# Cross-attention and routed experts on one Trainium2 core: where VectorE adds the residual in the third slot of a block

## What is computed

```python
def rms_norm(x, w):                       # over the last axis (head of 128)
    return w * x * rsqrt(mean(x * x) + 1e-6)
q = (layernorm(x) @ Wq).reshape(B, S, 16, 128)
k = (ctx @ Wk).reshape(B, S, 4, 128)
v = (ctx @ Wv).reshape(B, S, 4, 128)
q, k = rms_norm(q, q_norm_w), rms_norm(k, k_norm_w)
probs = softmax(q @ k.T / sqrt(128))      # four query heads share one key head
x = x + (probs @ v).reshape(B, S, 2048) @ Wo
xn2 = layernorm(x)                        # 8192 tokens
w, sel = top_2(softmax(xn2 @ gate_w.T))   # of 12 experts, capped list for each
for each expert e: h = silu((xs @ w1.T) * (xs @ w3.T)) @ w2.T; x[tokens] += w * h
```

## Time and profile before

| | |
|---|---|
| median of 3 runs | 2482.19 us (2481.06 to 2484.36) |
| the profiled execution | 2481.01 us, span 2479.1 us |
| PE busy | 2271.0 us, 92% of the span |
| DVE busy | 1869.0 us, 75% |
| ACT busy | 1766.7 us, 71% |
| POOL busy | 1125.1 us, 45% |
| mean granted TensorE clock | 0.961 |

### The profile page before, as it was taken

How to read it: one execution, slowest core, us unless ns; L and a number is a source line. 1 busy time by engine, 2 the same in 40 slices (tenths; PEclk the granted TensorE clock), 3 DMA queues, 4 the chain that set the end, 5 groups by cost and what they waited for, 6 DMA issues and landing times. The chain is left out here.

```text
span 2479.1 us, 54081 instructions
## 1 busy us (share of the span) xinstructions
PE 2271.0 (92%) x12931; PEld 1152.0 (46%) x12931; DVE 1869.0 (75%) x5158; ACT 1766.7 (71%) x6911; POOL 1125.1 (45%) x1949
## 2 busy tenths in 40 slices
PE   3899999999999999999999999999999999468884
PEld 1344444444444444444444444445444444244442
DVE  6778888888888888888888888888888887436554
ACT  5877777777777777777777777777777777234442
POOL 4334444444444444444444444444444443268875
PEclk9899999999999999999999999999999999778886
DMA  8477766666777667676676777667676766359997
GB/s 256 94 140 138 140 139 138 136 134 137 136 144 141 137 137 144 138 137 137 137 136 135 135 142 143 136 135 141 140 139 137 136 135 119 83 144 188 182 177 93
DMA packets 894363, 348.08 MB, mean 140 GB/s; under 512 B 829004, under 2 KB 829260, under 8 KB 894288
## 3 DMA queue, kind: packets, MB, share of 16 engines
q1 hardware_dynamic: 867520, 297.06, 60.3%
q0 software_dynamic: 22912, 43.16, 9.8%
q10 hardware_dynamic: 3888, 7.38, 0.8%
HBM read 91.37 MB, written 57.71 MB: 60 GB/s over the span
## 5 line engine op out<-in xcount | busy, mean ns | idle before, releaser
L824 PE MATMUL pb<-wo,o 128*128 128x512 f16 x3072 | 709.8, 381 | 61.6 <-DVE work L1164 50.3
L954 ACT ACTIVATE work<-pb,small 128x128 f32<-128x128 f32 x1024 | 455.2, 453 | 165.1 <-DVE small L1139 165.1
L1407 POOL TENSOR_TENSOR small<-small 128x4 f32<-128x4 f32 (+1 forms) x584 | 485.4, 835 | 54.0 <-POOL small L1478 13.8
L824 PEld LDWEIGHTS pb<-wo,o 128*128 128x128 f16 x3072 | 287.1, 98 | 397.5 <-issue 61.2
L1478 POOL TENSOR_TENSOR small<-small 128x4 f32<-128x4 f32 x256 | 84.2, 329 | 697.3 <-ACT junk_q L935 691.6
L755 PE MATMUL pb<-wq,xT 128*128 128x512 f16 x1536 | 356.4, 382 | 0.9 <-DVE q L1127 0.9
L755 PE MATMUL pb<-wq,wkv_raw 128*128 128x512 f16 x1536 | 352.4, 379 | 0.6 <-DVE q L1127 0.6
L1127 DVE SCALAR_TENSOR_TENSOR q<-pb,small,q 128x128 f16<-128x128 f32 x1024 | 288.3, 344 | 71.7 <-ACT q L944 71.7
L968 ACT ACTIVATE o<-pb 128x512 f16<-128x512 f32 x256 | 153.1, 598 | 222.4 <-PE pb L812 221.8
L944 ACT ACTIVATE q<-pb,small 128x128 f16<-128x128 f32 x1024 | 291.1, 365 | 4.6 <-DMA qT<-q 4.5
L935 ACT ACTIVATE junk_q<-pb 128x128 bf16<-128x128 f32 x1024 | 273.4, 305 | 6.4 <-PE pb L755 6.4
(11 more groups left out here) (152 smaller groups left out, 3546.1 us busy)
## 6 DMA issues: line engine op xcount, KB each, us to landing
work<-x SPq DMA_DIRECT2D x128, 256.0 KB, 3.0
work<-c SPq DMA_DIRECT2D x64, 256.0 KB, 4.0
out<-work SPq DMA_DIRECT2D x64, 256.0 KB, 2.1
xn_scratch<-work SPq DMA_DIRECT2D x64, 256.0 KB, 2.3
wo_raw<-wo ACTq DMA_DIRECT2D x4, 1024.0 KB, 9.1
qT<-q SPq DMA_TRANSPOSE x256
pT<-p SPq DMA_TRANSPOSE x256
wq_raw<-wq ACTq DMA_DIRECT2D x3, 1024.0 KB, 11.3
```

Source lines behind the costliest of these rows:

```text
L824: mm = nc.tensor.matmul(WO_B[:, :], o16[:, HPG * a + h, :], part(O0 + g, b_)[:, h, :], start=(g == 0 and h == 0 and n == 0), stop=(g == NG ...
L954: ex = nc.scalar.activation(probs[:, cols], S_B[:, cols], ACT.Exp, bias=nmax[:, h:h + 1], scale=esc, accum_out=psums[:, h:h + 1])
L1407: return nc.gpsimd.tensor_tensor(out_, in_, neghalf[:, 0:n], ALU.pow)
```

## The change

On DVE, in the third slot of a block (g 2), `residual(b - 1)` stands ahead of `norm_k(b + 1)` and so also ahead of `normalise(b, 2)`; before, it stood behind both. Nothing else is touched: the same instructions with the same waits, on DVE alone.

```diff
                         if g == 1 and live(b):
                             split_v(b)
+                        if g == 2 and live(b - 1):
+                            residual(b - 1)
                         if g == 2 and live(b + 1):
                             norm_k(b + 1)
...
                         if g == 1 and live(b + 2):
                             stats_x(b + 2)
-                        if g == 2 and live(b - 1):
-                            residual(b - 1)
                         if live(b):
                             split_p(*cur)
```

## The result

| | before | with the change |
|---|---|---|
| median of 4 runs | 2481.62 us (2480.93 to 2484.36) | 2422.28 us (2419.59 to 2425.45) |
| profiled execution, span | 2481.01, 2479.1 | 2425.45, 2423.6 |
| start of the last residual | 2144.38 | 2086.48 |
| from there to the end | 334.7 | 337.1 |

The ratio is 0.9759, with a 95% interval of 0.9742 to 0.9777: 59.3 us faster by the medians, 55 to 64 by the interval. The forecast was 57.5 us faster, at 2424.7, in a range of 2421 to 2437.

What follows compares the result with a forecast made beforehand. PE was taken to bound the attention stage; 52.2 us from 60 waits, 1.74 from block 1, 1.43 at the loop's end and 2.16 from block 63 sum to 57.5, giving 2424.7 us, range 2421 to 2437.

Steps and rivals of the forecast that it cites:

- PE's wait: Third slot, ahead of out_project: PE's wait for the residual goes, 0.87 us a pass, with 1.4 us to spare.
- How often: Of PE's 63 waits, 60 alike give 52.2 us; block 1 gives 1.74 and the slot at the loop's end 1.43.
- Block 63: Last block, without norm_k: the residual passes normalise alone and PE starts out_project 2.16 us earlier, all taken as won.
- lower end of the range: Block 63's out_project at full clock with less idle time ahead, 1.3 us more, and 1.2 us run spread: about 2422.
- The sum: Whole kernel: 52.2 + 1.74 + 1.43 + 2.16 = 57.5 us won, giving 2424.7 us against the median.
- ACT and DVE behind the residual: Third slot: L1148 and ACT's p cast 0.3 us later, k cast waits for norm_k, delays don't add; DVE still waits 0.3 us.
- Can DVE hold the faster pace?: DVE's own chain a pass: 30.63 us, 30.9 with the delay, against PE's 31.45; PE stays the bound with 0.5 to spare.
- The second rival: DVE becomes the bound as the third slot grows over 0.5 us more than reckoned; 2453 us, chance 0.12.
- Is the residual's own input there?: Load of x_res, issued at 1016.99, has landed by 1019.1, over 4 us ahead of the residual's new start at 1023.42.
- the fourth rival: At the third slot's head the residual waits for its load, holding up DVE's chain; slower, 2524 us in its example, chance 0.03.
- POOL beside DVE: POOL's factor chain will run beside norm_k and L1148; slowing of DVE taken as 0, with 1.0 us a pass as other end.
- The third rival: PE doesn't go faster without its pause, from instruction queue refill or a lower clock; 2482 us within 0.2%, chance 0.05.

Runs made afterwards that it cites:

- halved run: Kernel before, with the residual in its new place only in blocks with odd b, in its old place in the others; ratio 0.9872, pass 31.88 us.
- run with the POOL products: The change, with 16 small POOL products (128x1) added behind the factor chain of the third slot; ratio 0.9762, pass 31.45 us.
- run of n = 3: The change, with three more unread bn_stats operations (128x512) on DVE ahead of its third slot's last operation; ratio 0.9975, pass 32.27 us.

## Why the prediction was right, and where not

*PE's wait.* Right by its own numbers: 0.87 us a pass was forecast, and 32.32 - 31.45 is 0.87. The 1.4 us to spare can be read in the rows after: the residual ends at 997.41 + 0.74 = 998.15 and PE starts at 999.68, 1.53 us later, of which 0.15 is the distance kept where PE does wait. That the residual need only be in time is shown by the run in which it comes 1.03 us later at no cost. The run with one more DVE operation goes to the edge: in block 36 the load held the residual up 1.47 us, and PE started 0.20 us behind the small matmul, in place of 0.03:

```profile
1251.47 0.75 DVE L1167 SCALAR_TENSOR_TENSOR work<-pb,small,work 128x512 f32<-128x512 f32 x1 [1.47 <-DMA work<-x]
```
```profile
1252.17 0.17 PE L844 MATMUL pb<-macc,ones_b 128*128 128x24 bf16 x1
1252.37 2.75 PE L825 MATMUL pb<-wo,o 128*128 128x512 f16 x12
```

*How often.* The halved run shows that the waits add up one by one. Block 1 too: PE's `out_project` of its third slot came 19.37 us behind that of its first slot in the kernel before (102.40 to 121.77), and 17.62 us with the change (101.55 to 119.17), 1.75 against a forecast of 1.74.

*Block 63.* Its `out_project` follows that of block 62 at 29.23 us instead of 31.49, 2.26 us won against a forecast of 2.16. I took all of it as kept. In this profile 0.4 us are given back in the next slot:

```profile
2066.62 4.39 PE L824 MATMUL pb<-wo,o 128*128 128x512 f16 x12 [1.99 <-DVE work L1164]
...
2074.02 2.76 PE L824 MATMUL pb<-wo,o 128*128 128x512 f16 x12 [1.64 <-DVE o L1076]
```

The twelve matmuls take 4.39 us where they took 4.03, and it is 7.40 us to the next group, not 6.99. The granted clock over the twelve is 0.61, against 0.67 before; singly they take 0.38 us at the one level and 0.63 at the other. But this can't be put down to the change. Over the fourteen traces the same twelve take 4.03 to 5.28 us with the residual in its old place and 2.75 to 5.13 in the new one. The 2.75, at a clock of 1.00 and with 5.71 us to the next group, is in the run with the POOL products:

```profile
2067.70 2.75 PE L825 MATMUL pb<-wo,o 128*128 128x512 f16 x12 [1.99 <-DVE work L1165]
```

So the further 1.3 us that I put at the lower end of the range do occur, in one of nine traces, and the clock granted at this place moves the distance to the next group between 5.7 and 8.4 us, whatever the kernel.

*The sum.* By the two profiles the last residual is 57.9 us earlier. Of these 0.85 lie ahead of block 1 and are no work of the change; 57.05 are, against 57.5. The experts' stage took 2.4 us more in this profile, and so the spans differ by 55.5. It moves by itself: the two profiles and the twelve others put it at 322 to 337 us. The medians differ by 59.3 us, inside the same scatter.

*ACT and DVE behind the residual.* L1148 came 0.25 us later (0.3 forecast), and ACT's k cast waits 0.49 us for the keys. The two delays don't add, and DVE still waits for PE, 0.34 us (0.3 forecast).

*Can DVE hold the faster pace?* This is the step that was mis-sized: "32.32 - 1.69 = 30.63 us", and with the delay 30.9, with 0.5 us to spare. It is 30.4, with 1.0 to spare. I had taken the idle times in the brackets as all that DVE waits for PE. They leave out short ones: in the first slot DVE's `maxima` starts 0.77 us behind the start of L1071 x (1005.37, then 1006.14), and without a wait, in the runs where DVE is the bound, 0.60, yet there is no bracket. They also shorten long ones, since consecutive rows of DVE overlap. Compared from start to start with the run of n = 3, the four `maxima` of a pass wait 0.17, 0.05, 0.40 and 1.55 us in the kernel before (medians), 2.17 and not 1.69. So the chain there was 30.15, and with the 0.25 us of the new order it is 30.4. The second rival was less likely for it than the 0.12 that I gave. It erred to the safe side and moved nothing in the forecast.

*Is the residual's own input there?* This step failed: "so it has landed by then, over 4 us ahead of 1023.42", from a lull of the DMA engines in one window. In the trace of before, the loads of x_res land 2.8 to 7.7 us behind their issue, half of them over 4.7 us, by the times at which their last semaphore increment arrives (61 of the 64 have all their 16 increments on record). Even the load of that window landed at 1021.6, 4.6 us behind its issue and 1.8 ahead of 1023.42; the lull was not its end. The new place is 6.4 us behind the issue in this pass. Block by block, 6 loads of the trace before land behind the place where `norm_k` starts, by 0.1 to 1.3 us; with the change the residual waited in the three blocks of the view, by 0.87 us at most. Nor is it chance that a load is late, as the fourth rival had it: between any two of the ten traces with the load in this place the landing times block by block correlate (0.45 to 0.91), and blocks 14, 20, 24 and 36 are among the slowest six in 6 to 8 of them. It cost nothing, as both DVE's 1.0 us and PE's 1.4 us cover it; that luck, and not a landing by 1019.1, is what kept the fourth rival away.

*POOL beside DVE.* Right, now with a run of its own. The Trainium skill (SBUF — State Buffer, section SBUF: two separate sides) has the shared port pair as a lock for whichever comes first. The runs bear out the half by which POOL waits (L1478 takes 0.70 us beside L1071 k, 0.20 elsewhere, and a product 0.67 or 0.70 beside L1149 or L1072), and not, for products of 0.19 us, the half by which VectorE would: L1149 and L1072 started inside one and stayed at 0.69.

*The third rival* is out: PE runs 1010 us without a stop, at a granted clock of 1.00 throughout.

No run beat the change by more than its interval. The attention passes are now bound by PE alone, so another order on DVE has nothing to give; what is left is ahead of block 1 and behind block 62.

## What to carry to other kernels

On an engine that works through a fixed list, look for the short operation that the bounding engine waits for and that stands behind a wait for a third engine: moving it ahead of that wait can win the whole stall, and it is enough that it is in time. The price of the move is what everything behind it now waits for, so size the slack of its inputs by the slowest of all its executions and not by one window. Which engine is next, and how much it has to spare, is measured more surely by adding operations whose result nobody reads, until a pass grows, than read from brackets.

## What the runs showed that I had not expected

- A plain load of 256 KB, issued between transposes, landed 2.8 to 7.7 us behind its issue in one execution of the kernel. It is slower in the even blocks (5.4 us in the mean of the ten traces with the load in this place) than in the odd ones (4.5), which the other body of the loop runs. Issued one step later, behind the transpose of p, it took 2.8 to 4.6 us, median 3.0, and behind the transpose of q 2.5 to 3.6, median 2.7. These are the times of the last semaphore increment of each load. Why it is slow in the first place (its neighbour there is the load of the context, also 256 KB) wasn't tried, and neither was what makes the same blocks slow in each execution.
- The share of the experts' stage differed by 10 us between occasions (334.7 and 337.1 against 322 to 328 us), with a granted clock of 0.75 and 0.76 in the two profiles of the first, and 0.75 in one of 323.9 us of the second; the clock does not explain it, and what does stays open. The attention passes agreed to 0.01 us on both.
